# A mixture-of-experts layer on one core: 26 instead of 28 halvings, one-hots over seven blocks, expert loops written out

## What is computed

```python
xn = _layernorm(x, axis=-1)                      # x: 4 x 2048 x 512, float32
x = x + mixer(xn) + experts(xn)

def mixer(x):
    x_input, x_gate = split(x @ W_in.T)          # 1024 channels each
    u = silu(causal_conv4(x_input) + conv_b)
    h = scan(0.95 * h + 0.05 * (u @ W_B.T))      # 64 states, per sequence
    y = (h @ W_C.T + D_param * u) * silu(x_gate)
    return layernorm(y @ W_out.T + x, g, b)

def experts(x):                                  # 8192 tokens, 8 experts
    scores = (tanh(xf @ gate_w.T) + 1) * 0.5
    vals, idx = top_k(scores.T, 1024)            # each expert takes its 1024 best tokens
    y = layernorm(xf[idx])
    o = gelu(y @ fc1.T + b1) @ fc2.T + b2        # 512 -> 2048 -> 512
    return xf.at[idx].add(o * vals)
```

## Time and profile before

| | |
|---|---|
| median of 3 runs | 2662.08 us (2660.77 to 2664.01) |
| profiled execution | 2662.32 us |
| its span, first to last instruction | 2660.6 us |
| mean granted TensorE clock | 0.998 |
| TensorE busy | 2630.5 us (99% of the span), 11818 matmuls |
| VectorE busy | 2051.3 us (77%) |
| ScalarE busy | 1497.3 us (56%) |
| GpSimd busy | 671.4 us (25%) |
| stage 1 | 0 to 107.4 us |
| mixer blocks 0 to 15 | from 107.4 us, the last from 1225.35 us |
| loop over experts 1 to 6 | 1475.71 to 2478.39 us |

### The profile page before, as it was taken

The page is one execution under the profiler, slowest core; times in us unless marked ns, Lnnn a source line. Parts: engine busy times, 40 slices in busy tenths (PEclk is TensorE's granted clock), DMA queues, the critical chain, the costliest instruction groups (busy, mean ns, idle before and its releaser), DMA issues.

```text
span 2660.6 us, 41530 instructions
## 1 busy us (share of the span) xinstructions
PE 2630.5 (99%) x11818; PEld 2134.6 (80%) x11820; DVE 2051.3 (77%) x3525; ACT 1497.3 (56%) x2578; POOL 671.4 (25%) x1006
## 2 busy tenths in 40 slices
PE   8999999999999999999999999999999999999998
PEld 4588888888887788888888888888888888888886
DVE  8778888887887788888876767867688677786654
ACT  5744555555555565665545555565555655556553
POOL 5422222222222122223432214113141131311102
PEclk9999999999999999999999999999999999999999
DMA  9733222233333322225443425234252342533313
GB/s 371 254 127 111 91 89 87 92 91 103 111 111 111 111 75 87 87 94 161 151 134 110 114 72 142 77 95 131 64 145 81 95 131 64 138 89 91 100 52 71
DMA packets 139656, 299.95 MB, mean 113 GB/s; under 512 B 26224, under 2 KB 26352, under 8 KB 135664
## 3 DMA queue, kind: packets, MB, share of 16 engines
q1 hardware_dynamic: 105840, 201.54, 22.9%
q0 software_dynamic: 33664, 96.75, 14.9%
HBM read 244.46 MB, written 53.77 MB: 112 GB/s over the span
## 4 chain that ended last, share of the span: by engine, by line
PE 95%; DVE 2%; issue 1%; ACT 1%; DMA 0%; POOL 0%; SPq 0%; DVEq 0%; POOLq 0%; ACTq 0%
PE po L2516 9%; PE po L2518 9%; PE po L2517 9%; PE ring L1577 9%; PE ring L1578 9%; PE ring L1579 9%; PE pb L2516 4%; PE pb L2518 4%; PE pb L2517 4%; PE po L1615 4%; PE po L1616 4%; PE po L1617 4%; PE pc L2517 2%; PE pc L2518 2%; PE pc L2516 2%; PE pb L571 1%
## 5 line engine op out<-in xcount | busy, mean ns | idle before, releaser
L2516 PE MATMUL po<-w2h,hid_h 128*128 128x512 f32 x1024 | 402.1, 393 | 0.1
L1577 PE MATMUL ring<-xt_h,w_h 128*128 128x512 f32 x1024 | 400.0, 391 | 0.1
L2517 PE MATMUL po<-w2l,hid_h 128*128 128x512 f32 x1024 | 398.6, 389 | 0.0
L1578 PE MATMUL ring<-xt_l,w_h 128*128 128x512 f32 x1024 | 398.5, 389 | 0.0
L1579 PE MATMUL ring<-xt_h,w_l 128*128 128x512 f32 x1024 | 398.4, 389 | 0.0
L1372 DVE SCALAR_TENSOR_TENSOR u<-xin,cw,u 128x512 f32<-128x512 f32 x384 | 288.5, 751 | 74.2 <-issue 32.8
L1998 POOL DMA_INDIRECT out_dram<-res,idx_c x64 | 107.6, 1682 | 482.9 <-DVE res L2363 470.2
L1577 PEld LDWEIGHTS ring<-xt_h,w_h 128*128 128x128 f32 x1024 | 192.2, 188 | 40.9 <-DVE xt_l L542 0.9
L1579 PEld LDWEIGHTS ring<-xt_h,w_l 128*128 128x128 f32 x1024 | 192.2, 188 | 40.1
L2516 PEld LDWEIGHTS po<-w2h,hid_h 128*128 128x128 f32 x1024 | 192.3, 188 | 39.5 <-DVE hid_l L2353 0.5
L1578 PEld LDWEIGHTS ring<-xt_l,w_h 128*128 128x128 f32 x1024 | 192.3, 188 | 39.4
(11 more groups left out here) (298 smaller groups left out, 6301.9 us busy)
## 6 DMA issues: line engine op xcount, KB each, us to landing
w2r<-fc_in SPq DMA_DIRECT2D x256, 256.0 KB, 2.7
wo<-wo_halves POOLq DMA_DIRECT2D x120, 512.0 KB, 4.9
w1r<-fc_in SPq DMA_DIRECT2D x144, 256.0 KB
x_tail<-x_in SPq DMA_DIRECT2D x64, 256.0 KB, 2.8
out_dram<-res SPq DMA_DIRECT2D x64, 256.0 KB, 2.0
g_x<-x_in SPq DMA_DIRECT2D x15, 1024.0 KB, 8.5
xt_rows<-g_xnt SPq DMA_DIRECT2D x15, 1024.0 KB, 10.1
rows<-xt_rows SPq DMA_DIRECT2D x15, 1024.0 KB, 6.2
```

Source lines behind the costliest of these rows:

```text
L1577: pe.matmul(ring[r % 2][:, :], w_h[:, r, q], xt_h[:, k, :], start=(k == 0), stop=False)
L1578: pe.matmul(ring[r % 2][:, :], w_h[:, r, q], xt_l[:, k, :], start=False, stop=False)
L2516: pe.matmul(dst, ah, bh, start=start, stop=False, skip_group_check=more)
L2517: pe.matmul(dst, ah, bl, start=False, stop=False, skip_group_check=more)
```

## The change

One block fewer is searched; its last two rounds run at START and GAP of the prefix block. Prefix, slot and one-hot blocks move up by one, so the one-hot blocks are 8 to 14: four with five one-hots and three with four. On TensorE, VectorE and ScalarE the loop over experts 1 to 6 is written out by Python; SyncE and GpSimd keep theirs.

```diff
 ROUNDS = 4
-BISECT_BLOCKS = 7
-assert ROUNDS * BISECT_BLOCKS >= 26
+BISECT_BLOCKS = 6
+ALL_ROUNDS = ROUNDS * BISECT_BLOCKS + 2
+assert ALL_ROUNDS >= 26
...
-HOT_BLOCKS = 6
+HOT_BLOCKS = 7
 START, START_2, GAP, GAP_2 = -4, -3, -2, -1
-HOT_AT = 2 * ((START, 0, 1, 2, 3, 5),) + 4 * ((START, 0, 1, 3, 5),)
-PLACE_AT = 2 * ((0, 1, 1, 2, 4, 5),) + 4 * ((0, 1, 1, 3, 5),)
+HOT_AT = 4 * ((START, 0, 1, 3, 5),) + 3 * ((START, 0, 1, 3),)
+PLACE_AT = 4 * ((0, 1, 1, 3, 5),) + 3 * ((0, 1, 1, 3),)
...
         def prefix(c):
+            if c == START:
+                count(ALL_ROUNDS - 2)
+                halve(ALL_ROUNDS - 2, pc)
+                count(ALL_ROUNDS - 1)
+            if c == GAP:
+                halve(ALL_ROUNDS - 1, pc)
             if c == 1:
-                dve.wait_ge(c_thr, 2 * ROUNDS * BISECT_BLOCKS + 1)
-                dve.wait_ge(c_cnt, ROUNDS * BISECT_BLOCKS + 1)
+                dve.wait_ge(c_thr, 2 * ALL_ROUNDS + 1)
+                dve.wait_ge(c_cnt, ALL_ROUNDS + 1)
...
             if c == 0:
-                if type(b) is not int or b == 0:
+                if type(b) is not int or b in (0, PREFIX_BLOCK):
                     pe.wait_ge(c_gain, b * ROUNDS + 2 + 1)
...
         def prefix(c):
+            if c == START:
+                pe.wait_ge(c_y1, PREFIX_BLOCK * NC_ + 1)
+                tally(ALL_ROUNDS - 2, pc)
+            if c == START_2:
+                pe.wait_ge(c_gain, ALL_ROUNDS - 1 + 1)
+                tally(ALL_ROUNDS - 1, pc)
...
-        with act.Fori(1, E - 1) as e:
+        for e in range(1, E - 1):
             expert(e)
...
-        with dve.Fori(1, E - 1) as e:
+        for e in range(1, E - 1):
             expert(e)
...
-        with pe.Fori(1, E - 1) as e:
+        for e in range(1, E - 1):
             expert(e)
```

## The result

| | before | changed |
|---|---|---|
| median, 22 runs each | 2662.97 us | 2658.33 us |
| lowest to highest | 2660.77 to 2665.97 | 2656.49 to 2660.79 |
| ratio (95% interval) | | 0.9983 (0.9978 to 0.9989) |
| span of the profiled execution | 2660.6 us | 2658.8 us |

The changed kernel is 4.6 us faster, 0.17%. This is inside the 0.2% that a few runs can tell from nothing; the 44 runs here do tell it.

The account below looks back on a forecast made before the run. TensorE, busy 2630.5 of 2660.6 us, was taken as the bound. One-hots and rounds (-4.50 + 0.44 = -4.06) plus written-out expert loops (-0.98) gave -5.04 us: 2662.08 to 2657.0, range 2654.7 to 2660.3.

Parts of the forecast that it names:

- Part 1: One-hot mixer blocks: no one-hot at step 2 ends TensorE's waits for VectorE's late u_l; -4.50 us with one search block fewer.
- Part 2: Search and prefix blocks: two halving rounds disappear, two move into the prefix block and add 0.44 us, 0.22 each.
- the block's excess: Search block's 1.0 us over 320 matmuls at 0.2266, mostly its four rounds; counted from it, a round is 0.25 us.
- Part 3: Experts 1 to 6: written-out loops make all six passes 166.95 us, 1001.70 instead of 1002.68, so -0.98 us.
- ScalarE's late return: Expert passes, 13th matmul: ScalarE's bank copy comes late after a jump, TensorE waits; clearly late in two passes of five.
- Rival A: One-hot blocks or expert loops: a part of the gain does not come, 2658.0 to 2660.8 us; chance 0.09.
- Rival B: Written-out experts: fetching TensorE's 30 more instruction pieces becomes the bound, slower, up to 2674 us; chance 0.03.
- Rival C: Expert passes: smoother ScalarE and VectorE remove small restarts, or measurement lands low; over 0.2% won, 2655 to 2656.7 us; chance 0.35.

Follow-up runs that it names:

- list part: Kernel before with only the changed rounds and one-hot tables, all expert loops kept: median 2666.07 us against 2661.93, ratio 1.0014.
- list part moved back: The list part with 112 semaphore increments nobody waits for, moving TensorE's expert loop to seven pieces: 2658.42 us against 2662.80, ratio 0.9985.
- the run on stage 1: Changed kernel with the loops of stage 1 (score computation) also written out on all five engines: 2658.19 us against 2662.47, ratio 0.9982.

## Why the prediction was right, and what in it was not

**The time.** Forecast 2657.0 us from 2662.08, which is -5.04, and a range of 2654.7 to 2660.3; measured 2658.33, and a difference of -4.64 with an interval of -5.9 to -2.9. The traces behind stage 1 say -5.1. (The range's low end is 1.0 us below what its stated terms give, 2657.0 - 1.3 = 2655.7. Nothing hangs on it.)

**Part 1, one-hots.** Right in cause, place and size. The blocks of five last 74.93 (74.92 to 74.93) as forecast, those of four 74.44 instead of 74.49. The cause is shown by three runs, one profile each, against blocks that repeat to 0.03 us: the waits follow the table into later blocks, come back with five one-hots when one stands at step 2 (+1.07), and mostly go with six when none does (-1.6).

**Part 2, rounds.** The prefix block is 73.87 instead of 73.81. A round costs 0.25 us, the value from the block's excess, and not 0.22, the value from the timeline. Four-one-hot blocks and rounds miss in opposite directions, and the sum is off by 0.01.

**Part 3, the loops.** The number was right (-0.96 for -0.98), the account of it only for this pair of kernels. "TensorE's own jump costs nothing" was read from passes of a loop that happens to stay loaded. The list part moves the loop, from seven pieces to eight by the count, and then the jumps cost 1.05 to 1.28 us each, and the six passes are 6.4 us longer than straight code. With the lists changed and the loops kept, the time is 4.1 us over the kernel before; with the loops written out, 4.6 under it. (The lists with TensorE's loop alone written out were not run; that it is TensorE's loop rests on the two runs that moved it.) The two parts are not terms of a sum: alone they give +4.1 and -0.5 by their medians, together -4.6. So it is in part luck that the forecast came out: it knew nothing of the interaction, and the change happens to hold both of its sides. Had the loops been left alone, the same reasoning would have said -4.1 and been wrong in sign.

Against the kernel before, ScalarE's late return is shown to be the whole of the 0.98 (its loop alone gives 1001.72). But it is no constant: with ScalarE's loop at the same place in its stream, the runs have 0.98, 1.60, 0.60 and 0.09 us over 1001.7, and where the lists moved it, the copy is never later than 1.77 us into a pass (list part and list part moved back). With the new lists, then, ScalarE's loop would have cost nothing as it stood (one profile, that of the list part moved back), and what writing out the loops earns in this change is that TensorE's is not loaded again. Why some returns are late and others not was not settled. TensorE can do without the copy until about 1.9 us into a pass: copies at 1.90 or earlier cost nothing, one at 2.04 made a pass 0.16 us longer, one at 2.22 0.34 and one at 2.45 0.57. Straight code has it at 1.56.

**Rival A** (part of the gain stays away) did not come. **Rival B** looked for a price of TensorE's stream where the code is straight: 33 pieces more, against about 30 forecast, cost nothing. The price exists, and it is paid by the loop. Its own argument, that pass 1 is straight code and the shortest, holds wherever the loop stays loaded (no pass of any run is under 166.95); in the list part alone pass 1 takes 168.00, its end being the first late jump. **Rival C**: nothing beyond the sum is in the traces.

**The scatter.** The forecast said a median of three might be off by 1.3 us. Block 0 starts between 106.5 and 110.7 us in the 14 profiles, while mixer blocks of the same code agree to 0.1 us but for block 1 (above). The scatter is made in stage 1, in its first block above all: 7.8 to 10.7 us from the first score matmul to the second block's. The expectation of the run on stage 1 looked for late instruction pieces or loads, but the 14 profiles also fall into two groups. In eight the granted clock is 0.50 for 3.41 us at 18 to 23 us, and block 0 starts at 108.3 to 110.7; in six it stays at 1.00, and block 0 starts at 106.5 to 107.4. TensorE was idle for 2.1 to 3.4 us ahead of the place in the eight, and for 1.2 to 2.3 in the six.

## What to carry to other kernels

Before calling a loop's jump free or the instruction stream harmless, look at the instruction queues in the second pass of the loop: if pieces of the engine's own queue arrive in every pass, the loop does not stay loaded, and an edit ahead of it can push it over that edge or back. Time a part of a change by itself before crediting it. And where an engine that is not the bottleneck feeds the one that is, the order of its extra work against those feeds is worth more than its amount: a one-hot moved by a step cost 1.07 us, a one-hot more without a wait 0.44 to 0.71.

## What the runs showed of the hardware that was not expected

- TensorE's instructions arrive in 16 KB packets on queue 8. A loop of 1671 instructions is loaded once or, moved by 128 instructions, again in each pass (8 or 9 pieces), with TensorE idle for 0.8 to 1.8 us at each jump. By the count it touches seven pieces in the first case and eight in the second.
- ScalarE and VectorE load again behind each jump of loops of 400 and 497 instructions (the prediction's 333 for ScalarE leaves out its 66 waits): queue 14 brings 9 to 11 pieces in such a pass and 5 in one of straight code. VectorE's first operation came 3.8 to 4.4 us into the passes of the kernel before, against 0.95 in straight code, and ScalarE's up to 2.5, against 1.56.
- After 1.83 us without a matmul the granted clock fell from 1.00 to 0.51 for about 3.4 us in one pass; after a gap of 1.79 us three passes later it did not. In stage 1 it fell for 3.41 us behind gaps of 2.1 to 3.4 us in eight profiles, and stayed behind one of 2.26 us in another.
